# Attention between two FFNs: score products dealt over the array in another way, groups half as long, queries kept resident

## The reference

```python
x = x + 0.5 * ffn(layernorm(x), w_gate, w_up, w_down)   # FP4-quantised inputs and weights, 704 hidden
x = x + attn(layernorm(x), Wq, Wk, Wv, Wo, We)
x = x + 0.5 * ffn(layernorm(x), w_gate, w_up, w_down)
# attn: 16 heads of 16 features, S = 4096
ctx = X @ We.T                                           # 32 features
scores = Q K^T / 4 + 0.1 * (ctx ctx^T)                   # per head; the second term is shared by all heads
out = softmax(scores) V, heads joined, @ Wo.T
```

## Time and profile before

| | us |
|---|---|
| median of 3 runs | 3794.17 |
| the profiled execution | 3794.98 |
| its span, first to last instruction | 3793.2 |
| PE busy | 3656.0 (96%) |
| DVE busy | 3114.7 (82%) |
| ACT busy | 2533.1 (67%) |
| POOL busy | 1104.9 (29%) |

### The profile page before, as it was taken

The page is one execution under the profiler, slowest core; times in us unless marked ns, Lnnn a source line. Parts: engine busy times, 40 slices in busy tenths (PEclk is TensorE's granted clock), DMA queues, the critical chain, the costliest instruction groups (busy, mean ns, idle before and its releaser), DMA issues. The chain is left out here.

```text
span 3793.2 us, 79235 instructions
## 1 busy us (share of the span) xinstructions
PE 3656.0 (96%) x28132; PEld 2466.6 (65%) x28132; DVE 3114.7 (82%) x5241; ACT 2533.1 (67%) x4811; POOL 1104.9 (29%) x906
## 2 busy tenths in 40 slices
PE   3998799999999999999999999999999999999799
PEld 2897466666666666666666666666666666665698
DVE  7996688888888888888888888888888888885798
ACT  4764376666777766666777666676666666766465
POOL 3990112222222222222222222121222222222597
PEclk9999799999999999999999999999999999999899
DMA  3004511212121212121212121212121212122000
GB/s 131 18 20 158 128 38 40 47 41 48 40 48 41 48 39 49 40 49 40 49 40 49 40 48 40 49 40 49 40 48 41 48 41 45 41 51 79 35 19 23
DMA packets 310556, 187.61 MB, mean 49 GB/s; under 512 B 197440, under 2 KB 240864, under 8 KB 309216
## 3 DMA queue, kind: packets, MB, share of 16 engines
q1 hardware_dynamic: 304688, 179.88, 21.3%
q10 hardware_dynamic: 5552, 3.44, 0.4%
HBM read 144.54 MB, written 33.55 MB: 47 GB/s over the span
## 5 line engine op out<-in xcount | busy, mean ns | idle before, releaser
L1313 DVE TENSOR_REDUCE tops<-coarse 128x1 f32<-128x512 f32 x4069 | 2485.1, 683 | 496.7 <-PE coarse L1200 496.5
L1302 ACT ACTIVATE x_all<-fine 128x512 f32<-128x512 f32 x4096 | 2063.0, 625 | 789.8 <-PE fine L1214 789.0
L1214 PE MATMUL fine<-query_a,key_a 64*128 64x512 f32 x4096 | 1576.2, 428 | 0.3
L1214 PE MATMUL fine<-query_b,key_b 33*128 33x512 f32 x4096 | 1493.0, 394 | 2.8 <-DMA query_b<-neg_max 2.8
L1214 PE MATMUL fine<-query_c,key_c 64*128 64x512 f32 x4096 | 1482.0, 391 | 0.0
L1200 PE MATMUL coarse<-key_a,max_query 64*128 64x512 f32 x4069 | 1432.1, 420 | 21.8 <-DMA max_query<-scratch_c_query 13.5
L1200 PEld LDWEIGHTS coarse<-key_a,max_query 64*128 64x128 f32 x4069 | 715.6, 186 | 522.8 <-DVE tops L1313 226.7
L1223 PE MATMUL o_ps<-x_all,vh 128*32 128x512 f32 x8192 | 984.8, 598 | 0.0
L1214 PEld LDWEIGHTS fine<-query_a,key_a 64*128 64x128 f32 x4096 | 753.0, 185 | 77.2 <-ACT x_all L1302 11.1
L1214 PEld LDWEIGHTS fine<-query_b,key_b 33*128 33x128 f32 x4096 | 753.5, 184 | 75.5 <-DMA query_b<-neg_max 5.6
L1214 PEld LDWEIGHTS fine<-query_c,key_c 64*128 64x128 f32 x4096 | 756.7, 185 | 42.6
(11 more groups left out here) (193 smaller groups left out, 2650.1 us busy)
## 6 DMA issues: line engine op xcount, KB each, us to landing
query_c<-scratch_c_query SPq DMA_DIRECT2D x256, 128.0 KB, 2.7
query_a<-scratch_q_hi SPq DMA_DIRECT2D x512, 32.0 KB, 1.8
query_a<-scratch_c_query SPq DMA_DIRECT2D x256, 64.0 KB, 2.0
query_b<-neg_max SPq DMA_DIRECT2D x1024, 0.5 KB, 2.0
max_query<-scratch_q_hi SPq DMA_DIRECT2D x508, 32.0 KB, 1.8
max_query<-scratch_c_query SPq DMA_DIRECT2D x254, 64.0 KB, 2.0
query_b<-scratch_q_lo SPq DMA_DIRECT2D x256, 32.0 KB, 2.4
x_all<-in_L_attn_X SPq DMA_DIRECT2D x4, 1024.0 KB, 12.4
```

Source lines behind the costliest of these rows:

```text
L1214: return pe.matmul(fine[i % 2][:, r, :], keys[rows, cols], query[rows, :], start=chunk == 0, stop=chunk == CHUNKS - 1)
L1302: act.activation(probs[:, i % RING, r, :], fine[i % 2][:, r, :], ACT.Exp).then_inc(probs_ready, 1)
L1313: dve.tensor_reduce(tops[n][:, idx // KB, idx % KB:idx % KB + 1], bank, AX.X, ALU.max).then_inc(tops_ready, 1)
```

## The change

- A tile's rows are dealt as 49, 64 and 32: keys (32 rows of context, 16 rows q_hi k_hi, the maximum's row), positions (64 rows, as before), and low (16 rows q_lo k_hi, 16 rows q_hi k_lo). A 32-row product takes one quarter of the array. Two tiles of one half take five places in the order instead of six: in the third place stand the low products of both, each in its own quarter of the half.
- Groups have two pairs instead of four: eight groups a step, each of seven waves (`WAVES`), then `times_v` over four key tiles. There are four coarse products in a group, at the first, third, fourth and seventh wave.
- The coarse product has 48 rows and uses `query_a`; `max_query` is gone. `query_a` and `query_c` hold all 4096 queries; the context rows are loaded once. A step loads two 16-row pieces of q_hi for step s+3 and four pieces of `query_b`; eight small DMAs of the maxima go to `query_a`. Key loads of the next head are spread over six steps, one piece (one DMA) in each.
- SyncE's loop over the steps is written out in full instead of a loop with registers. The scratch of Q and K is laid out by head.
- Weights phase: `front(1)` goes ahead of the splits of v and o, `front(2)` ahead of e; the right half of the down weights' back operations goes to GpSimd, the left half stays on VectorE; one block of statistics moves ahead of two splits.

```diff
+                pool.wait_ge(step_ready, 4)
+                pool.tensor_tensor(xn[2][:, RIGHT], xn[2][:, RIGHT], step_sb[2][:, RIGHT], ALU.add).then_inc(back_chain, 1)
+                pool.wait_ge(back_chain, 5)
+                pool.tensor_tensor(xn[2][:, RIGHT], xn[2][:, RIGHT], step_sb[2][:, RIGHT], ALU.subtract).then_inc(back_chain, 1)
+                pool.wait_ge(back_chain, 6)
+                pool.tensor_tensor(blocks_of(raw[2][:, RIGHT]), blocks_of(xn[2][:, RIGHT]), spread(right_scale, IP // BLK), ALU.mult).then_inc(down_back, 1)
...
                 front(0)
-                for u in range(0, 3):
+                for u in range(0, 2):
                     split(u)
                 front(1)
-                for u in range(3, 5):
+                for u in range(2, 4):
                     split(u)
                 front(2)
+                split(4)
                 statistics(0)
                 dve.wait_ge(step_ready, 3)
-                dve.tensor_tensor(xn[2][:, :], xn[2][:, :], step[2], ALU.add).then_inc(down_chain, 1)
+                dve.tensor_tensor(xn[2][:, LEFT], xn[2][:, LEFT], step[2][:, LEFT], ALU.add).then_inc(down_chain, 1)
                 dve.wait_ge(down_chain, 1)
-                dve.tensor_tensor(xn[2][:, :], xn[2][:, :], step[2], ALU.subtract).then_inc(down_chain, 1)
+                dve.tensor_tensor(xn[2][:, LEFT], xn[2][:, LEFT], step[2][:, LEFT], ALU.subtract).then_inc(down_chain, 1)
                 dve.wait_ge(down_chain, 2)
-                dve.tensor_tensor(blocks_of(raw[2][:, :]), blocks_of(xn[2][:, :]), spread(scale[2], NB[2]), ALU.mult).then_inc(down_back, 1)
+                dve.tensor_tensor(blocks_of(raw[2][:, LEFT]), blocks_of(xn[2][:, LEFT]), spread(scale_sb[2][:, 0:IP // BLK], IP // BLK), ALU.mult).then_inc(down_back, 1)
                 for u in range(5, 7):
                     split(u)
                 statistics(1)
+                statistics(2)
                 for u in range(7, 9):
                     split(u)
-                statistics(2)
                 statistics(3)
...
-GROUP = 4
+GROUP = 2
...
-WAVES = ["CCfffCfffCffffff", "ffffffCfffCfffCC"]
+WAVES = ["CffCfff", "ffCfffC"]
 CHUNKS = 3
+TWO_TILES = ["position", "keys", "low", "position", "keys"]
...
 def group_of_waves():
 
-    waves, tiles, products, ended = [], [0, 0], [0, 0], []
-    count = 0
+    waves, ended, products, steps, count = [], [], [0, 0], [0, 0], 0
     for k in range(len(WAVES[0])):
         wave = []
         for r in range(2):
             if WAVES[r][k] == "C":
-                wave.append((r, None, products[r], count))
+                wave.append((r, None, "coarse", products[r], count))
                 products[r] += 1
                 count += 1
-            else:
-                tile, chunk = divmod(tiles[r], CHUNKS)
-                wave.append((r, tile, chunk, None))
-                tiles[r] += 1
-                if chunk == CHUNKS - 1:
-                    ended.append((tile, r))
-        waves.append(sorted(wave, key=lambda item: item[1] is None or item[2] == 0))
+                continue
+            two, at = divmod(steps[r], len(TWO_TILES))
+            steps[r] += 1
+            if at < CHUNKS:
+                wave.append((r, 2 * two, TWO_TILES[at], at, None))
+            if at >= CHUNKS - 1:
+                wave.append((r, 2 * two + 1, TWO_TILES[at], at - CHUNKS + 1, None))
+        wave.sort(key=lambda item: item[1] is None or item[3] == 0)
+        ended += [(tile, r) for r, tile, what, at, order in wave if tile is not None and at == CHUNKS - 1]
+        waves.append(wave)
     return waves, ended
...
-UNITS_IN_GROUP = len(WAVES[0]) * 2 - 2 * GROUP * CHUNKS
+UNITS_IN_GROUP = 2 * WAVES[0].count("C")
...
+        def load_heads_queries(eng, s, loaded):
             for r in range(2):
+                eng.dma_start(query_a[half_rows(r, DE, DK), tokens(s)].bitcast(F32), scratch["q"][s // NQB, 1, :, tokens(s)]).then_inc(loaded[s % 2], 16)
...
+                def load_queries_b(s):
+                    for part in range(4):
+                        sp.dma_start(query_b[s % 2][part * LOW:(part + 1) * LOW, :].bitcast(F32),
+                                     scratch["q"][s // NQB].rearrange("two d t -> (two d) t")[:, tokens(s)]).then_inc(qb_loaded[s % 2], 16)
...
+                for piece in range(2, KEY_PIECES):
+                    load_keys(0, 0, piece)
+                load_query_positions(sp, slice(2 * QB, T), qc_loaded[1])
+                for r in range(2):
+                    sp.dma_start(query_c[half_rows(r, 0, HALF), :].bitcast(F32), scratch["c_query"][DE:DE + HALF, :]).then_inc(qc_loaded[1], 16)
+                load_heads_queries(sp, 2, qa_loaded)
+                for piece in range(KEY_PIECES):
+                    load_keys(1, 1, piece)
                 load_max(0, 0)
 
...
+                        load_heads_queries(sp, s + 3, qa_loaded)
+                    if s >= 2:
...
+                        load_queries_b(s + 1)
...
+                        load_max(s + 1, (s + 1) % 2)
+
+                for s in range(STEPS):
+                    step(s)
+                    head, block = divmod(s - 2, NQB)
+                    after, piece = divmod(s - 1, NQB)
+                    if 0 < after < H - 1:
+                        load_keys((after + 1) % 2, after + 1, piece)
...
+                def coarse_product(bank, t, keys, q, r, kb):
+                    first = t % NQB * QB + q * P
+                    return pe.matmul(bank, query_a[half_rows(r, 0, M_ROW), first:first + P],
+                                     key_a[keys][half_rows(r, 0, M_ROW), kb * 512:(kb + 1) * 512], start=True, stop=True)
...
+                def score_chunk(s, half, kp, i, r, what, at):
+
+                    cols, queries = slice(i * P, (i + 1) * P), tokens(s)
+                    if what == "low":
+                        rows, part = half_rows(r, i % 2 * LOW, LOW), slice(i // 2 * P, (i // 2 + 1) * P)
+                        keys, query = key_b[kp][rows, part], query_b[half][rows, :]
+                    elif what == "keys":
+                        rows = half_rows(r, 0, M_ROW + 1)
+                        keys, query = key_a[kp][rows, cols], query_a[rows, queries]
+                    else:
+                        rows = half_rows(r, 0, HALF)
+                        keys, query = key_c[rows, cols], query_c[rows, queries]
+                    return pe.matmul(fine[i % 2][:, r, :], keys, query, start=at == 0, stop=at == CHUNKS - 1)
```

More of the change, by code:

```diff
@@ L151, in weights_phase @@
         step = [step_sb[0][:, :], step_sb[1][:, :], step_ps[:, :]]
-        scale = [scale_sb[0][:, :], scale_sb[1][:, :], small_ps[:, 384:384 + NB[2]]]
+        scale = [scale_sb[m][:, :] for m in range(3)]
+        LEFT, RIGHT = slice(0, IP), slice(IP, 2 * IP)
+        right_scale = scale_sb[2][:, IP // BLK:2 * IP // BLK]
         X_LOADS = 4
@@ L997, in attention_phase @@
         sb = lambda name, shape, dt=F32: ctx.enter_context(nc.sbuf_tensor(name, shape, dt))
-        key_a, key_b = [[first, sb(f"key_{name}1", [P, T // 2], F32R)] for first, name in zip(first_keys, "ab")]
+        key_a, key_b = [first_keys[0], sb("key_a1", [P, T // 2], F32R)], [first_keys[1], sb("key_b1", [P, T // 4], F32R)]
         key_c = sb("key_c", [P, T // 2], F32R)
-        query_a, query_b, query_c = [[sb(f"query_{part}{n}", [P, QB], F32R) for n in range(2)] for part in "abc"]
-        max_query = [sb(f"max_query{n}", [P, QB], F32R) for n in range(2)]
+        query_a, query_c = [sb(f"query_{part}", [P, T], F32R) for part in "ac"]
+        query_b = [sb(f"query_b{n}", [P, QB], F32R) for n in range(2)]
+        ones = sb("ones", [1, P])
         vh = [sb(f"vh{n}", [P, KT, 32]) for n in range(2)]
@@ L1060, in _ @@
             def _(pool):
[L1061 to L1068, removed]
+                pool.memset(ones[:, :], 1.0).then_inc(filled, 1)
                 link = Chain(pool, v_filled)
@@ L1122, in load_max @@
                             for j in range(QT):
-                                sp.dma_start(query_b[n][half_rows(r, M_ROW, 1), j * P:(j + 1) * P].bitcast(F32),
+                                first = s % NQB * QB + j * P
+                                sp.dma_start(query_a[half_rows(r, M_ROW, 1), first:first + P].bitcast(F32),
                                              neg_max[n][:, j:j + 1].bitcast(F32)).then_inc(m_loaded[n], 16)
-                load_keys_a(0, 0)
+                for r in range(2):
+                    load_keys_a(0, 0, r)
@@ L1140, in _, with step @@
+                load_heads_queries(sp, 2, qa_loaded)
+                for piece in range(KEY_PIECES):
+                    load_keys(1, 1, piece)
                 load_max(0, 0)
-                def step(s, half, before_last, last):
+                def step(s):
                     sp.wait_ge(probs_ready, P_LEAD + TILES * s)
-                    if within(s + 1):
-                        load_operand_a(sp, 1 - half, query_a, s + 1, q_loaded)
```

(31 more changed lines are left out.)

160 lines of the change are left out of this document (68 added, 92 removed).

## The result

The changed kernel takes 7162.06 us in the median of four runs (7135.62 to 7371.63) against 3794.14; a fifth run took 7088.85. The ratio is 1.8807, 95% interval 1.8694 to 1.8919, over the fast runs alone, which leave out the profiled one of 7371.63 us (mean clock 0.708 against 0.734 to 0.745). The forecast was 3637, range 3580 to 3870. The rows of the profiled run serve for what stands beside what; its sum is some 210 us above the median.

A forecast was written before the change was run, and what follows sets the result against it. TensorE was taken to set the pace in attention, with VectorE second. From 3794.98 us profiled, -154 (steady steps), +2 (start) and -5 (weights) gave 3638, so 3637 for the median, range 3580 to 3870.

The forecast's parts named there:

- the price the trace doesn't show: Waves 4 and 5 of each group: changing to and from 32-row products, taken as 0, upper end +1.3 to +1.9 us.
- The rival: Waves 4 and 5 of each group: array empties at each change between 64 and 32 rows, 5000 to 5600 us; chance 0.07.
- The steady step: Attention: two new groups take 5.65 us against 5.95, -154 us in all, a step 22.6, VectorE and ScalarE hidden.
- Rivals 3 and 4: Attention groups: 3, VectorE still runs dry, 4150 to 4400, chance 0.03; 4, 0.14 us wait returns, 3780, no separate chance.
- rival 2: Waves 4 and 5: a wave's third product costs 0.1 us, 3842 in full (chance 0.05), 3740 at half.
- theory C: Waves 4 and 5: the third product in a wave costs, not the change of shape; no separate chance given.
- V's second turn: Attention, per old group: one more change to V and back +0.31 us, the wait for VectorE gone -0.14.
- Start: Start of attention: larger loads of queries and positions delay it, +2 us, range 0 to +6.
- Weights: Weights phase: ends near 50.5 us instead of 55.2, -5 us, range -7 to 0.

The follow-up runs named there:

- e2_one32: Changed kernel with the second tile's low product left out, the first tile's still 32 rows; 4914.09 us, ratio 1.295.
- e3_aligned: Complete changed kernel with only the order changed, so the low products of both halves stand in one wave; 4066.64 us, ratio 1.0717.
- e5_order: Complete changed kernel with only waves 4 and 5 issued in another order, four changes of shape instead of six; 4709.29 us, ratio 1.2411.
- e4_third32: Kernel before with each tile's third product at 32 rows instead of 33 (maximum's row left out, exponential scaled by 0.01); 8487.74 us, ratio 2.2367.
- e1_one64: Changed kernel with the first tile's low product on all 64 rows of its half and the second tile's left out; 3654.17 us, ratio 0.963.
- e7_groups2: Kernel before with groups of two pairs alone, eight waves a group and V after each; 3864.07 us, ratio 1.0184.
- e10_layout: e1_one64 with scratch of Q and K laid out high or low part outermost, so saves write 128 rows in one dimension; 3629.94 us, ratio 0.9569.
- e8_weights: Kernel before with the changed kernel's weights phase and nothing else; 3791.36 us, ratio 0.9992.

## Why the prediction was wrong

- **The step that failed** is "the price the trace doesn't show": "I take 0". The timeline above gives about 0.19 us for each change (0.1 before it, 0.1 in the piece after it) and 0.235 for each piece that no longer runs beside another. Six changes and three more pieces are +1.85 us, 4.68 a group at the full clock instead of 2.83 (4.72 in the stretch above), +1894 us over 1024 groups. The same two prices give 4.06 for e2_one32 (four changes, two pieces; measured 4.05), 3.21 for e3_aligned (two, none; 3.22) and 3.83 for e5_order (four, one; 3.83), and e4_third32 makes the case with one row, 10.76 us a group at the full clock against 5.95.
- **The evidence was there.** The gaps around V and the loads that nothing made ahead were read, priced rightly (six gaps, 0.33 to 0.43, +1.3 to +1.9 us a group) and set aside with an argument: V changes columns too, and the low products lie in rows which their half has just left. Neither is of the trace. A product in rows 64 to 127 holds up one in rows 0 to 63, if only its shape is another.
- The Trainium skill, TensorEngine Tiling (Array Packing), Tiling Modes, Key Properties, says that a change of the tiling mode drains TensorE; the runs agree, 0.42 instead of 0.235 us from start to start where rows alone change. It says next that different tiles can load weights and multiply in parallel; the x4 of e3_aligned agrees, for tiles of one shape only. The prediction had also weighed the XBUS picture in the Trainium skill, TensorE: Matmul & The Clock Gate, Part 2, by which row tiling takes no extra streaming buses and column tiling does. No run shows the buses, and V's is not the dearer kind: its change and the one back are 0.31 us by the earlier trace rows, two changes of rows 0.38.
- **The rival was underpriced too**: 5000 to 5600, measured 7162. The sum at the full clock is 3637 + 1894 + 26 (the start, 28 less the 2 that 3637 holds) = 5557. The missing 1605 goes with the clock, 0.69 in attention: the rival's text took rows at the upper level only, the two levels' groups of 4.72 and 8.19 us give the mean group within 0.04, and e5_order, with the same products at 0.99, has no such remainder. That the clock takes it is shown; why it falls is not.
- **The steady step besides was right**: 22.56 us against 22.6 (e1_one64), VectorE's and ScalarE's banks hidden, SyncE in time. Rivals 3 and 4 fell with e1_one64; rival 2 (theory C) fell with e2_one32, 1.2 us a group too slow with no third product in a wave, and with e3_aligned, where four pass like one.
- **V's second turn**: +0.31 less 0.14 forecast by parts; e7_groups2 measured +0.14 an old group (70 / 512) where +0.17 follows.
- **Start**: +2 forecast, range to +6; about +28 in the changed kernel and +25 in e1_one64 (first coarse product at 438.8 and 435.1 against 414.3, with the weights' 4 added). The forecast counted the loads and passed over the layout of the scratch, a part of the change that the prediction did not speak of; e10_layout gives 24 of it back. The loads, which the +2 was for, added nothing.
- **Weights**: -5 forecast. In the changed kernel's trace the last split ends at 51.1 instead of 55.2: -4.

```profile
40.62 1.49 POOL L231 TENSOR_TENSOR raw<-w_xn,w_scale 128x768 f32<-128x768 f32 x1
...
49.58 1.54 DVE L240 TENSOR_TENSOR gu_lo<-w_ps,gu_hi 128x640 fp32r<-128x640 f32 x2
```

GpSimd's third operation ends at 42.1, 1.1 later than the 41 taken, and TensorE starts on it at once (42.16); that covers the 0.6 by which the end misses the 50.5 worked out. In its median e8_weights shows 3 of the 4, and its interval takes in no change at all.

## What to carry to other kernels

A product of 32 rows did not overlap with one of 48 or 64 in any run here, not even in the other half of the array, while products of 33, 48 and 49 rows ran beside those of 64; keep equal shapes together in time, and count the changes as well as the products. If a trace shows that one change of shape has a price, take that price for every other kind until a run says otherwise. And when products stop running side by side, ask of the clock too: here it cost nearly as much again as the gaps.

## What the runs showed that I had not expected

- The clock of attention fell with six changes a group (0.69), and in the kernel before with sixteen to its group of twice the length (0.67), and not with four (0.99 to 1.00); 4 more products in one half took it from 0.69 to 0.51, 4 more pairs to 0.80.
- Taking one row of 33 away more than doubled the time of the kernel before.
- Four 32-row products into four banks pass in the 0.44 us of one.
- Writing 256 KB as 8 by 16 rows instead of 128 rows went with 184 instead of 239 GB/s for the projection's DMAs, and with a start of attention 23 us later.
